# Linear mixtures of experts: dense gate and up against tokens sorted by expert through DRAM, down turned token-major

## The reference

```python
def _moe_linear(x, router_w, expert_w):
    n_exp = router_w.shape[0]
    logits = x @ router_w.T
    vals, idx = jax.lax.top_k(logits, K)
    probs = jax.nn.softmax(vals, axis=-1)
    onehot = jax.nn.one_hot(idx, n_exp, dtype=x.dtype)
    combine = jnp.einsum('tk,tke->te', probs, onehot)
    out = jnp.zeros((x.shape[0], expert_w.shape[1]), x.dtype)
    for e in range(n_exp):
        out = out + combine[:, e:e + 1] * (x @ expert_w[e].T)
    return out
g = _moe_linear(xt, router_gate, w_gate)
u = _moe_linear(xt, router_up, w_up)
inter = jax.nn.silu(g) * u
d = _moe_linear(inter, router_down, w_down)
```

## Time and profile before

| what | us |
|---|---|
| time, median of 3 runs | 2822.8 (2820.82 to 2824.21) |
| span of the profiled execution | 2821.3 |
| TensorE busy in the span | 2566.3 (91%) |
| VectorE, ScalarE, GpSimd busy | 1636.3, 1263.8, 531.0 |
| first stage of feed-forward 2 | from 1859.84 to 2212.28 |
| window attention | 2212.3 to 2288.4 |
| second stage of feed-forward 2 | from 2288.39 to 2646.55 |

### The profile page before, as it was taken

One profiled execution on the slowest core, in us unless ns is written; L12 is line 12 of the kernel. 1 busy time (PEld: TensorE's weight loads), 2 busy tenths in 40 slices (PEclk: granted clock), 3 DMA queues, 4 the chain that ended last, 5 costly groups with the idle time before them and its releaser, 6 DMA issues. The chain is left out here.

```text
span 2821.3 us, 39708 instructions
## 1 busy us (share of the span) xinstructions
PE 2566.3 (91%) x13383; PEld 1283.0 (45%) x13472; DVE 1636.3 (58%) x2746; ACT 1263.8 (45%) x2914; POOL 531.0 (19%) x571
## 2 busy tenths in 40 slices
PE   7989999987986899999999978889999879999988
PEld 3446666654883222222222238844444634444433
DVE  5778888855224888888888612243332433333454
ACT  3662333333653587888887855521100321111343
POOL 1235666521235200000000013310000000000112
PEclk9988999999997799999999979999999889999999
DMA  2353223201572220110200017741221022120212
GB/s 98 95 154 102 85 99 100 85 23 68 168 205 63 63 41 14 22 32 4 41 14 3 3 59 243 218 138 58 70 80 49 12 69 84 60 90 31 64 43 61
DMA packets 132363, 212.55 MB, mean 75 GB/s; under 512 B 17969, under 2 KB 84273, under 8 KB 129425
## 3 DMA queue, kind: packets, MB, share of 16 engines
q1 hardware_dynamic: 128104, 202.08, 24.4%
q0 software_dynamic: 4096, 8.40, 0.9%
HBM read 177.22 MB, written 32.89 MB: 74 GB/s over the span
## 5 line engine op out<-in xcount | busy, mean ns | idle before, releaser
L2798 DVE TENSOR_REDUCE big<-psum 128x2 f32<-128x1024 f32 x512 | 604.0, 1221 | 76.7 <-PE psum L2595 72.6
L2752 ACT ACTIVATE probs<-psum 128x512 f32<-128x512 f32 x1024 | 553.3, 600 | 143.4 <-PE psum L2616 128.5
L2616 PE MATMUL psum<-big,k_ops 128*128 128x512 bf16 x944 | 294.6, 386 | 13.2 <-ACT probs L2752 6.7
L1509 PE MATMUL psum<-big 128*128 128x512 f32 x512 | 231.6, 603 | 18.0 <-DVE big L1642 18.0
L2616 PEld LDWEIGHTS psum<-big,k_ops 128*128 128x128 bf16 x1024 | 81.1, 97 | 335.2 <-ACT probs L2752 259.2
L1534 PE MATMUL psum<-probs,big 128*128 128x512 f32 x512 | 222.0, 594 | 5.3 <-issue 3.6
L1523 PE MATMUL psum<-big 128*128 128x512 f32 x512 | 224.4, 594 | 0.0
L1859 POOL TENSOR_TENSOR big<-big 128x512 f32<-128x512 f32 x32 | 40.5, 1270 | 905.8 <-ACT big L1824 864.9
L1287 ACT ACTIVATE hidden<-psum,big 128x128 f32<-128x128 f32 x480 | 136.1, 375 | 126.4 <-PE psum L1187 91.1
L2595 PE MATMUL psum<-big,w_A_or_L_A 32*128 32x512 bf16 x1024 | 164.1, 398 | 25.7 <-DVE big L2798 14.1
L1341 DVE TENSOR_TENSOR probs<-psum,big 128x128 f32<-128x128 f32 x120 | 34.2, 289 | 220.2 <-PE psum L1200 177.3
(11 more groups left out here) (465 smaller groups left out, 3712.6 us busy)
## 6 DMA issues: line engine op xcount, KB each, us to landing
big<-row_store SPq DMA_DIRECT2D x96, 512.0 KB
big<-in_experts SPq DMA_DIRECT2D x120, 322.0 KB
big<-step_rows SPq DMA_DIRECT2D x16, 1024.0 KB
qkv_chunks<-big SPq DMA_DIRECT2D x48, 256.0 KB, 2.3
big<-qkv_chunks SPq DMA_DIRECT2D x16, 768.0 KB
big<-since_rows SPq DMA_DIRECT2D x32, 256.0 KB
big<-row_store SPq DMA_DIRECT2D x32, 256.0 KB, 5.1
slots<-slot_rows SPq DMA_DIRECT2D x24, 256.0 KB
```

The source lines that it names most:

```text
L1509: mm = pe.matmul(k.bank[4 + c % 2][:, :], w["gate"][:, e, c, :], scaled[:, e, :], start=(e == 0), stop=(e == E - 1))
L2616: pe.matmul(k.bank[2 + m % 3][:, :], k_ops[:, g % 2, h, kt * P:(kt + 1) * P], q_ops[:, g % 2, i % QB, h, :], start=True, stop=True).then_i ...
L2752: act.activation(probs[:, kt % 2, h, :], k.bank[2 + m % 3][:, :], ACT.Exp, scale=SCALE).then_inc(expd.sem, 1)
L2798: dve.tensor_reduce(into, k.row_pair[hp].rearrange("p (h t) -> p h t", h=2), AX.X, ALU.max).then_inc(row_max.sem, 1)
```

## The change

Feed-forward 2's function is replaced by `sorted_linear_ffn`. For each block and each of the two routers (gate and up) the pairs of token and expert, 1024 of them, are sorted by expert into 15 tiles of 128 places. GpSimd scatters the tokens' rows of 512 bytes to DRAM (`linear_rows`, 16 indirect transfers of 64 KB a block). SP brings them back in groups of up to four tiles (`bring_slots`); TensorE turns each tile (L1690), ScalarE copies the group (L1846), and one 128x128 by 128x512 matmul a tile makes all 512 outputs of its expert (`expand`, L1705, 30 a block, over banks 3, 4 and 5). ScalarE moves each result into a ring of six buffers (`evict`, L1854), SP stores it (256 KB, `store`), and GpSimd gathers the rows of 2 KB back to token order, 16 transfers of 256 KB a block, into two buffers (`gather`, L1661). ScalarE and VectorE mix the two rows of a token (`scale_gate` L1858, `mix`), ScalarE takes the Silu (L1863), VectorE multiplies (`multiply`), TensorE turns the product (`turn_inter`, L1719) and ScalarE copies it (`out_inter`, L1867). The mixing of block n stands among the tiles of the block behind it.

Down stays dense, but the tokens are now the stationary operand: per tile of 128 tokens and half of the experts four matmuls of 512 columns give four experts' results token by token, and VectorE sums them with a column of weights (`use_down`, 32 operations of 128x128 a block). TensorE turns the sum (`turn_y`, L1731) and VectorE adds it to x once a block.

The stage's blocks run in the order of `PHASES`. The stage before it and the window attention host more of its start: norm 0 and 1, routing, sorting, and the scatter of block 0, which GpSimd does ahead of the barrier. Layer 2's down weights are stored in another order, and the opening clears four more arrays of 960 KB in DRAM.

```diff
...
+    def pool_scatter(self, pool, n):
+        k = self.k
+        pool.wait_ge(self.placed.sem, self.placed.at(n))
+        pool.wait_ge(self.tokens_out.sem, self.tokens_out.at(n))
+        for r in range(ROUTERS):
+            for i in range(2):
+                for j in range(TPB):
+                    pool.indirect_dma_start(k.linear_rows[r][n % 2][:, :], self.row(n, r, i, j),
+                                            k.desk.tokens[:, n % 2, j, :], None).then_inc(self.put[r][n % 2].sem, 16)
...
+        elif self.stage == "L2":
+            self.route.pool_scatter(pool, 0)
...
+            if linear:
+                ahead.pool(pool)
...
+def sorted_linear_ffn(k, w, loads=(), begun=None, follows=None, left=None):
+
+    nc, C, HALVES, RING = k.nc, 4, 2 * TPB, 6
+    TILES = ROUTERS * SLOT_TILES
+    PHASES = (("expand", 0), ("expand", 1), ("down", 0), ("expand", 2), ("down", 1), ("expand", 3), ("down", 2), ("down", 3))
+    DOWN_BANK = (6, 7, 3, 4, 5, 6, 7, 6)
+    BANK_LAST = {5: 0, 6: 1, 7: 5}
...
```

```diff
...
+        def mixing(n):
+            if n == 0:
+                return {}
+            first = 11 if n == 1 else 4
+            return {first + 5 * j: (n - 1, j) for j in range(TPB)}
...
+            def store(n, m):
+                i = n * TILES + m
+                r, t = divmod(m, SLOT_TILES)
+                if m == 0 and n > 1:
+                    for j in range(2):
+                        sp.wait_ge(gathered[j].sem, dma(gathered[j], 8 * (n - 1)))
+                sp.wait_ge(evicted.sem, evicted.at(i))
+                sp.dma_start(k.linear_y[r][n % 2][t * P:(t + 1) * P, :], ring[:, i % RING, :]).then_inc(stored[i % RING].sem, 16)
...
+            def gather(n, j, r):
+                if j < 2:
+                    for i in range(RING):
+                        upto = [t for t in range(SLOT_TILES * (r + 1)) if t % RING == i]
+                        pool.wait_ge(stored[i].sem, dma(stored[i], n * TILES // RING + len(upto)))
+                if 4 * n + j > 1:
+                    pool.wait_ge(inter_turned.sem, inter_turned.at(4 * n + j - 2))
+                for i in range(2):
+                    pool.indirect_dma_start(back[:, j % 2, 2 * r + i, :], None, k.linear_y[r][n % 2][:, :],
+                                            route.row(n, r, i, j)).then_inc(gathered[j % 2].sem, 16)
...
+            def gather_block(n):
+                for j, r in ((0, 0), (1, 0), (0, 1), (1, 1), (2, 0), (2, 1), (3, 0), (3, 1)):
+                    gather(n, j, r)
...
+            scatter(1)
+            if left:
+                left.gather(pool)
+            gather_block(0)
+            for n in range(2, NB):
+                scatter(n)
+                gather_block(n - 1)
+            gather_block(NB - 1)
...
+            def experts_of(n, r):
+                pe.wait_ge(route.placed.sem, route.placed.at(n))
+                pe.load(k.pe_tile_regs, d.tile_expert[0:1, n, r * 16:r * 16 + SLOT_TILES])
+                return [pe.snap(reg, min_val=0, max_val=EXPERTS - 1) for reg in k.pe_tile_regs]
...
+            def expand(n, m, expert):
+                i = n * TILES + m
+                r, t = divmod(m, SLOT_TILES)
+                q = group_of(n, r, t // 4)
+                if t % 4 == 0:
+                    pe.wait_ge(slots_out.sem, slots_out.at(q))
+                if i > 2:
+                    pe.wait_ge(evicted.sem, evicted.at(i - 3))
+                if m < 3 and n > 1:
+                    pe.wait_ge(down_used.sem, down_used.at((n - 2) * HALVES + 2 + m))
+                if left and i == 2:
+                    pe.wait_ge(left.added.sem, left.added.at(NB - 2))
+                pe.matmul(k.bank[3 + i % 3][:, :], turned[:, q % 2, t % 4, :],
+                          w["up" if r else "gate"][:, bass.ds(expert * TB, TB)], start=True, stop=True).then_inc(made.sem, 1)
...
+            def down(n, q):
+                j, half = divmod(q, 2)
+                if half == 0:
+                    pe.wait_ge(inter_out.sem, inter_out.at(4 * n + j))
+                if q in BANK_LAST:
+                    pe.wait_ge(down_used.sem, down_used.at(n * HALVES + BANK_LAST[q]))
+                elif n > 0:
+                    pe.wait_ge(down_used.sem, down_used.at((n - 1) * HALVES + {0: 7, 1: 6}.get(q, q)))
+                if q == 2:
+                    pe.wait_ge(evicted.sem, evicted.at(min(n + 2, NB) * TILES - 1))
+                for c in range(C):
+                    mm = pe.matmul(k.bank[DOWN_BANK[q]][:, :], inter[:, n % 2, c, j * P:(j + 1) * P],
+                                   w["down"][:, c, half * TB:(half + 1) * TB], start=(c == 0), stop=(c == C - 1))
+                mm.then_inc(down_made.sem, 1)
+
...
+            def evict(n, m):
+                i = n * TILES + m
+                act.wait_ge(made.sem, made.at(i))
+                if i >= RING:
+                    act.wait_ge(stored[i % RING].sem, dma(stored[i % RING], i // RING))
+                act.activation(ring[:, i % RING, :], k.bank[3 + i % 3][:, :], ACT.Copy).then_inc(evicted.sem, 1)
...
+            def use_down(n, q):
+                j, half = divmod(q, 2)
+                from_bank = k.bank[DOWN_BANK[q]]
+                dve.wait_ge(down_made.sem, down_made.at(n * HALVES + q))
+                if q == 0 and n > 0:
+                    dve.wait_ge(y_turned.sem, y_turned.at(n - 1))
+                for e in range(4):
+                    share = down_route.comb[:, j, 4 * half + e:4 * half + e + 1]
+                    here = from_bank[:, e * D:(e + 1) * D]
+                    dve.drain()
+                    if half == 0 and e == 0:
+                        last = dve.tensor_scalar(y[:, j, :], here, share, None, ALU.mult)
+                    else:
+                        last = dve.scalar_tensor_tensor(y[:, j, :], here, share, y[:, j, :], ALU.mult, ALU.add)
...
-        ahead = follows(k, st, later=0, norm_later=0, banks=(7,), centre_bank=6, bank=7)
-
-        @block.sync
-        def _(sp):
-            ahead.sp_keep(sp)
-            ahead.sp_bring(sp)
+        ahead = follows(k, junk_st, later=0, norm_later=0, banks=(7, 7), centre_bank=6, bank=7, token_bank=6)
+
+        @block.gpsimd
+        def _(pool):
+            ahead.pool(pool)
...
             turn(3)
             ahead.pe(pe, "logits")
+            ahead.pe(pe, "tokens")
             add_up(3)
             ahead.pe(pe, "by_token")
+            pe.wait_ge(ahead.route.tokens_out.sem, ahead.route.tokens_out.at(0))
+            ahead.second.pe_centre(pe, 1)
             ahead.pe(pe, "turn")
+            pe.wait_ge(ahead.route.placed.sem, ahead.route.placed.at(0))
+            ahead.second.pe_variance(pe, 1)
+            ahead.second.pe_spread(pe, 1)
...
```

875 lines of the change are left out of this document (543 added, 332 removed).

## The result

In the first comparison the changed kernel took 2897.5 us, the kernel before 2821.8: a ratio of 1.0275 (95% interval 1.0256 to 1.0294), slower, where 2712 was forecast. A second comparison, on chip 12, gave the same: 2896.7 against 2819.7, ratio 1.0277 (1.026 to 1.0294). A third, on chip 3, gave the other sign with the same program: 2739.9 against 2793.6, ratio 0.9813 (0.9793 to 0.9833), faster by 1.9%. Of the five chips whose numbers are known, chip 12 has the kernel before at 2820 and the changed one at 2897; chips 0, 3, 11 and 15 have the kernel before at 2791 to 2799 and every kernel with the changed stages at 2737 to 2766.

The account below looks back on a forecast made before the run. Both mixture stages were taken as bound by TensorE's own work. Gains of 61.9 us in stage 1 and 48.5 in stage 2, together 110.4, taken from 2822.8 gave 2712 us; range 2672 to 2785.

Parts of the forecast that it names:

- What must keep up with it: Both mixture stages: other engines and DMA mostly hidden behind TensorE; GpSimd 40 and DMA 42 us of a block's 72.
- the stores bind: Rival, expansions: store landings of 7.5 us make a tile take 1.42 us, +57, total 2770; chance 0.06.
- Start of stage 1: First mixture stage: block 0's scatters behind earlier gathers put the first tile at 1862.9 against 1859.84, +3 us.
- the sum: Main forecast, both mixture stages: TensorE's work plus waits and start delays, gain 110.4 us, total 2712; chance 0.64.
- Stage 1: First mixture stage: 263.5 TensorE, 12 coupling, 5 chains, 3 late gathers, 4 leftover mix; 287.5 us against 352.4.
- Stage 2: Second mixture stage: 263.5 TensorE, 12 coupling, 5 chains, 3 late gathers, 6 hosted steps; 289.5 us against 358.2.
- the loads: TensorE's register loads, two a block: 0.7 us each beyond the queued tile, 5.6 us a stage, between 0 and 13.
- the coupling with ScalarE and VectorE: Three expansions a stage: hand-overs where ScalarE has no slack, charged 12 us a stage, bounded by 0 and 36.
- Window attention: Before the second mixture stage: routing, placing and 16 unhidden scatters start that stage at 2308.6 against 2288.39, +20.2 us.
- Clock: Rival, expansions: TensorE's granted clock falls to 0.81, 31.7 us more a stage, total 2775; chance 0.12.
- ScalarE as the bound: Rival, mixing expansions: evictions cost 0.60 us and mixing steps wait in line, total 2760; chance 0.12.
- GpSimd: Rival, both mixture stages: 2 KB-row gathers cost 4.1 us each, 385 us or more a stage, about 2905; chance 0.06.

Follow-up runs that it names:

- the late chip: Unedited changed kernel against the kernel before, on the slower kind of chip (or session), chip 12: 2896.7 us against 2819.7, ratio 1.0277.
- the pings: Changed kernel plus TensorE-ScalarE tile hand-overs and repeated 256 KB SP stores beside the window attention's 16 scatters; both together 2898.9 us on the late chip.
- the calm chip: Unedited changed kernel against the kernel before, on the other kind of chip (or session), chip 3: 2739.9 us against 2793.6, ratio 0.9813.
- run 47: Not a follow-up run: "run" is a verb here, and the mixing expansions of the changed kernel last 47, 46 and 37 us on the calm chip.

## Why the prediction was wrong

**The step that failed: "What must keep up with it", and the rival "the stores bind" at 0.06.** I compared GpSimd's and the DMA engines' loads with the period (40 and 42 us of 72), found room, and took landings from the earlier trace rows for stores beside bursts of eight indirect transfers. The step put what a long run does to the other engines at nothing. The change makes one run of 16 and others of 20 to 28 in a row, where the kernel before has eight at most. On the late chip the three phases under the long runs then take 25 + 23 + 11 us more than on the calm one in the first stage, 62 with the rest of it, and the second stage 55 more; ScalarE copies a bank up to 22 us after TensorE has filled it. The place and the sign are those of that rival, where it said slower from landings of 8.9 us; the mechanism is not, because ScalarE is late where it waits for TensorE alone, TensorE is slow where it waits for nothing, and no store is needed.

What makes them late is not settled. It isn't bandwidth (DMA share 0.29 to 0.57 there), nor a run of 16 scatters by itself (the pings). It goes with the chip, and with runs that hold scatters, not with short runs of gathers beside stores (expansion 3); whether the scatters, their number or the length of the run counts is open.

One rival is untested: the recording of the profile itself. The late profiles lack semaphore events just there: in 2004 to 2055 the trace holds 52 events of landings, the calm one 445 for the same phase, while beside the 16 scatters of the window attention, where nothing was late, it is 237 against 272. Of the late page's 240 stores of `linear_y` none has a time to landing, on the calm page their median is 3.1. Each timed execution has a span and a granted clock of its own, so no time on record is known to be free of the recorder. It may be that the recording suffers from the same cause, or that it is the cause; these runs can't tell.

**The stage ahead.** With the 16 scatters behind its gathers, a run of 24, it is stretched as well. Windows over it, changed kernel on the late and on the calm chip:

```profile
...
1670.00:1876.00 206.00, 158.41 (x1194) 144.70 (x1194) 49.78 (x190) 96.79 (x291) 61.68 (x64) 0.85 0.62 188
...
```

```profile
...
1650.00:1819.00 169.00, 147.12 (x1196) 135.35 (x1195) 49.83 (x190) 96.77 (x291) 50.87 (x53) 0.92 0.73 224
...
```

It takes 206 us against 182 before on the late chip, 169 against 168 on the calm one. I had priced these scatters by issue alone, +3 in all; the first tile came 23.5 us later (1883.36 against 1859.84).

On the late chip the stages run from 1883.36 to 2253.3 and from 2350.95 to 2720.3. The balance is: start +23.5, stage 1 369.9 against 352.4, window attention 97.7 against 76.1, stage 2 369.4 against 358.2, so 23.5 + 17.5 + 21.6 + 11.2 = +74 for a forecast of -110; the spans differ by 70.

**Point by point on the calm chip**, where the mechanism can be read without lateness. The page, and the ends of the stages:

```profile
span 2738.7 us, 41433 instructions
...
PE 2422.7 (88%) x13424; PEld 1228.6 (45%) x13424; DVE 1642.4 (60%) x2954; ACT 1454.2 (53%) x3263; POOL 782.2 (29%) x828
...
```

```profile
...
1843.45 2.07 PE L1705 MATMUL psum<-big,turned 128*128 x2 [1.04 <-ACT turned L1846]
```

```profile
...
2150.87 0.69 DVE L1966 SCALAR_TENSOR_TENSOR x<-psum,x 128x512 f32<-128x512 f32 x1 [0.75 <-PE psum L1731]
...
```

```profile
...
2249.22 2.07 PE L1705 MATMUL psum<-big,turned 128*128 x2 [1.06 <-ACT turned L1846]
```

```profile
...
2562.78 0.69 DVE L1966 SCALAR_TENSOR_TENSOR x<-psum,x 128x512 f32<-128x512 f32 x1 [0.75 <-PE psum L1731]
```

The kernel before on chip 11 starts its first stage at

```profile
...
1825.42 1.19 PE L1509 MATMUL psum<-big 128*128 128x512 f32 x1 [8.60 <-DVE big L1642]
```

and by its own rows ends it at 2178.45, starts the second at 2253.53 and ends it at 2612.50.

- Start of stage 1: 1843.45 against 1825.42, +18.0 for a forecast of +3. I took the cover from the late profile, where the stage ahead ended late at 1851; on the calm chip it ends at 1817, while the scatters' end is set by GpSimd's issue. And the first tile comes 10.2 us behind the 16 scatters (the last starts at 1832.04, plus a pitch of 1.25), where the sum had 5.5. Right mechanism; the cover and the way from the last scatter to the first tile were mis-sized.
- Stage 1: 308.1 against 353.0 us, forecast 287.5. Stage 2: 314.3 against 359.0, forecast 289.5. Of the 20.6 us that stage 1 is over its forecast, 13 are busy time: TensorE is busy 270.9 us in 1843 to 2151, against 258 from the sum without the loads. The amount of work was right and the clock was not, which the sum had at 1.00 throughout: granted was 0.95, and 258/0.95 is 271.6 (the first tile, behind an idle time, takes 2.07 us). Down was right: 28 us a block, full. The other 7.6 us are idle time, 37.2 against the 29.6 of all the sum's waits and loads. The mis-sized term among them is the coupling with ScalarE and VectorE, 12 us by the sum: waits for the product alone are 20.5. So the expansions that mix run 47, 46 and 37 us for 35.5, 33.9 and 31.8.
- Window attention: 97.7 against 75.1, +22.6 for a forecast of +20.2. Right.
- Gain 49 of these parts, 51.6 by the spans, for 110. Without lateness the sum had the sign and half of the size. That 2739.9 lies inside the stated range doesn't bear out the sum: the terms for the start, the coupling and the clock were each too small.

**The other rivals.** Clock: it fell, to 0.95 in both stages on the calm chip and not to the rival's 0.81. In expansion 2 (0.89) it did so where TensorE waited 3.48 and 2.09 us for the product. Expansion 3 stays at 1.00 with a wait ahead of every tile and waits of up to 1.9 us, so the Trainium skill's rule ("TensorE: Matmul & The Clock Gate", "A second HAM failure mode: psum-queue depth-cycling") isn't borne out in that phase; the other phases don't separate cycled banks from these longer waits. ScalarE as the bound: by it a gain of 63 us, nearer to the 54 measured on chip 3 than the sum's 110, though ScalarE is busy only 31 of 47 us there and it is the chain through it that binds. GpSimd: a gather of 2 KB rows costs what one of 512-byte rows does. The terms of this rival add up, as listed, to 405 us a stage and not to 385, which by its own reckoning is about 2945 in place of 2905; neither came true. Stores land in 3.1 us by the median with rare long ones. The rows (calm chip, gathers, then stores):

```profile
...
L1661 POOL DMA_INDIRECT big<-linear_y,linear_row x128: 940/946/1760, 1888.5 to 2516.3; - x128
...
DMA to landing us min/median/max: 3.2/5.0/8.7
```

```profile
...
L1624 SPq DMA_DIRECT2D linear_y<-big x240: 319/320/1619, 1846.2 to 2487.4; - x120
...
DMA to landing us min/median/max: 2.0/3.1/10.7
```

## What to carry to other kernels

A profile holds only as far as its pattern of load does: on the late chip stages with up to eight indirect transfers in a row were 14 and 15 us longer than on a calm one, those with 20 to 28 in a row 55 and 62, and the sum had no term for it. Ask for a replaced resource not only whether it has time in the period but how long its unbroken runs become, and who waits for a signal meanwhile. When a change leans on something new for the kernel, compare on more than one chip before believing either sign.

## What the runs showed of the hardware that I had not expected

Chips (or sessions on them) differ in a way that one program shows and another nearly hides: with 48 scatters and 64 gathers in each mixture stage the same kernel took 2740 us on one chip and 2897 on another, 5.7%, where the kernel before differed by 1%. On the late chip ScalarE copied a bank 22.3 us after TensorE had filled it while GpSimd issued a run of 28 indirect transfers, in a phase with a DMA share of 0.29, and four matmuls without a wait between them took 8.1 us in place of 3.70; whereas a ping between the two engines beside 16 scatters kept 0.84 us a round. In the first stage and the one ahead of it, the waits ended 4 us after the last transfer of a run was issued (1935.56, 2026.91 and 1865.96). An indirect transfer of 128 rows cost GpSimd 0.95 us for rows of 512 bytes and of 2 KB alike.
